# The order of TensorE's work on a strip: products and row sums in runs of four chunks instead of a change of kind with every chunk

## The reference, cut to what matters

```
XB = h @ B.T
x1 = x + tanh([h, t] @ W1 + b1) @ W2 + b2 + adj @ XB - rowsum(adj) * XB
```

## Time and profile before

| what | value |
|---|---|
| median of 3 runs | 904.75 us (904.72 to 905.37) |
| the profiled execution | 904.73 us |
| its span, first to last instruction | 903.5 us |
| TensorE matmuls busy | 776.9 us, 86% |
| VectorE busy | 729.3 us, 81% |
| DMA | 281.58 MB, mean 312 GB/s over the span |
| mean granted TensorE clock | 0.941 of full speed |

### The profile page before, as it was taken

One profiled execution on the slowest core, in us unless ns is written; L12 is line 12 of the kernel. 1 busy time (PEld: TensorE's weight loads), 2 busy tenths in 40 slices (PEclk: granted clock), 3 DMA queues, 4 the chain that ended last, 5 costly groups with the idle time before them and its releaser, 6 DMA issues.

```text
span 903.5 us, 13331 instructions
## 1 busy us (share of the span) xinstructions
PE 776.9 (86%) x5222; PEld 266.7 (30%) x5222; DVE 729.3 (81%) x958; ACT 128.5 (14%) x212; POOL 173.4 (19%) x160
## 2 busy tenths in 40 slices
PE   3898999999999999999999999999999999940000
PEld 1333232333333333333332323233333333320000
DVE  5889968989898989898989898998989897952111
ACT  2424011111111111111010201111111111110000
POOL 1000302020110202020202020202011020217774
PEclk9999999999999999999999999999999999985555
DMA  9797879697979797979798897979797979502221
GB/s 375 280 428 288 321 291 422 271 424 288 425 288 426 284 429 280 429 291 418 319 390 364 345 410 300 420 290 422 289 421 287 425 283 429 214 11 40 60 49 41
DMA packets 37267, 281.58 MB, mean 312 GB/s; under 512 B 14336, under 2 KB 18560, under 8 KB 20736
## 3 DMA queue, kind: packets, MB, share of 16 engines
q1 hardware_dynamic: 33152, 277.12, 74.9%
q0 software_dynamic: 4096, 4.20, 2.0%
HBM read 277.10 MB, written 4.19 MB: 311 GB/s over the span
## 4 chain that ended last, share of the span: by engine, by line
PE 74%; POOL 7%; DVE 5%; issue 4%; DMA 4%; SPq 4%; ACT 0%; POOLq 0%; DVEq 0%
PE acc L726 44%; PE row_sums L734 22%; POOL gathered L367 7%; DMA ring<-in_adj_t 4%; SPq L255 4%; DVE max_hi L514 2%; PE ps_hid L754 2%; PE ps_feat L796 1%; PE ps_xb L775 1%; PE ps_acc L768 1%; PE ps_turn L782 1%; PE ps_acc L771 1%; PE ps_acc L773 1%; PE ps_turn L789 1%; DVE max_lo L513 0%
## 5 line engine op out<-in xcount | busy, mean ns | idle before, releaser
L726 PE MATMUL acc<-ring,x_pb 128*64 128x512 f32 x2048 | 462.8, 601 | 18.4 <-DMA ring<-in_adj_t 18.4
L513 DVE TENSOR_TENSOR max_lo<-max_lo,ring 128x2048 f32<-128x2048 f32 x96 | 220.6, 2298 | 44.7 <-DMA ring<-in_adj_t 44.2
L734 PE MATMUL row_sums<-ring,ones_cols 128*32 128x512 f32 x2048 | 240.0, 597 | 0.0
L726 PEld LDWEIGHTS acc<-ring,x_pb 128*64 128x64 f32 x2048 | 141.0, 138 | 326.1 <-issue 326.1
L514 DVE TENSOR_TENSOR max_hi<-max_hi,ring 128x2048 f32<-128x2048 f32 x96 | 219.7, 2289 | 0.0
L358 POOL DMA_INDIRECT cand<-in_adj,cls_row x64 | 78.0, 1218 | 663.5 <-DVE cls_row L543 648.9
L734 PEld LDWEIGHTS row_sums<-ring,ones_cols 128*32 128x32 f32 x2048 | 56.5, 109 | 151.6 <-issue 149.8
L367 POOL DMA_INDIRECT gathered<-feats_dram,best x64 | 62.8, 981 | 19.5 <-issue 19.5
L651 DVE TENSOR_TENSOR gathered<-gathered,bias_row 128x512 f32<-128x512 f32 x8 | 5.6, 703 | 67.5 <-DMA gathered<-feats_dram,best 67.5
L508 DVE TENSOR_TENSOR max_lo<-ring 128x2048 f32<-128x2048 f32 x16 | 36.7, 2292 | 4.4 <-DMA ring<-in_adj_t 2.5
L510 DVE TENSOR_TENSOR max_hi<-ring 128x2048 f32<-128x2048 f32 x16 | 36.6, 2288 | 4.2 <-DMA ring<-in_adj_t 3.9
(11 more groups left out here) (95 smaller groups left out, 423.3 us busy)
## 6 DMA issues: line engine op xcount, KB each, us to landing
ring<-in_adj_t SPq DMA_DIRECT2D x128, 2048.0 KB, 11.3
x_tq<-in_x SPq DMA_DIRECT2D x1, 2048.0 KB, 30.8
feats_dram<-feats SPq DMA_DIRECT2D x16, 128.0 KB, 2.3
out<-gathered SPq DMA_DIRECT2D x8, 256.0 KB
x_pb<-in_x SPq DMA_DIRECT2D x1, 1536.0 KB, 7.8
cand<-in_adj,cls_row POOLq DMA_INDIRECT x64
gathered<-feats_dram,best POOLq DMA_INDIRECT x64
x_pb<-in_x SPq DMA_DIRECT2D x1, 512.0 KB, 4.6
```

The lines of the kernel that those rows point to most:

```text
L513: dve.tensor_tensor(max_lo[:, :], max_lo[:, :], lo, ALU.max).then_inc(lo_done, 1)
L726: last = pe.matmul(acc[parity][at:at + D, :], x_pb[:, c * CB + b, :], slot(c)[:, b * W:(b + 1) * W], start=(c == 0 and b < 2), stop=(c == ...
L734: last = pe.matmul(row_sums[at:at + QUAD, :], ones_cols[:, :], slot(c)[:, b * W:(b + 1) * W], start=(c == 0 and b < 4), stop=(c == NC - 1 ...
```

## The change

Only the program of TensorE changes. In strips 1 to 15 it takes the kinds in runs: products of chunks 0 and 1; `turn_maxima` and `turn_sums`; sums of 0 to 3; products of 2 to 5; `turn_h1`; sums of 4 to 7; `features` and `mlp_hidden`; products of 6 and 7, next to which stand those of the next strip's 0 and 1. The wait for a chunk's arrival becomes a function of its own. A chunk is released to SP (`pe_chunk`) when its second use is issued and done, still in the order of the chunks. Strip 0 keeps its order. The loads, SP's queue, VectorE, ScalarE and GpSimd are as they were.

```diff
+            def arrived(s, c):
                 pe.wait_ge(chunk_in[c % RING], s * (16 * NC // RING) + 16 * (c // RING + 1))
+            def products(c, parity):
...
             def strip(s, parity):
-                for c in range(NC):
-                    if c == 1:
-                        turn_maxima(s - 1)
-                        turn_sums(s - 1)
-                    chunk(s, c, parity)
-                    if c == 4:
-                        turn_h1(s - 1, ps_turn)
-                    if c == 5:
-                        features(s - 1)
-                        mlp_hidden(s)
+                for c in (0, 1):
+                    arrived(s, c)
+                    products(c, parity)
+                turn_maxima(s - 1)
+                turn_sums(s - 1)
+                pe.wait_ge(rows_copied, s)
+                for c in (0, 1):
+                    sums(c).then_inc(pe_chunk, 1)
+                for c in (2, 3):
+                    arrived(s, c)
+                    sums(c)
+                for c in (2, 3):
+                    products(c, parity).then_inc(pe_chunk, 1)
+                for c in (4, 5):
+                    arrived(s, c)
+                    products(c, parity)
+                turn_h1(s - 1, ps_turn)
+                for c in (4, 5):
+                    sums(c).then_inc(pe_chunk, 1)
+                for c in (6, 7):
+                    arrived(s, c)
+                    sums(c)
+                features(s - 1)
+                mlp_hidden(s)
+                for c in (6, 7):
+                    products(c, parity).then_inc(pe_chunk, 1)
```

More of the change, by code:

```diff
@@ L718, in turn_first @@
                 last.then_inc(pro_turned, 1)
-            def products(s, c, parity):
+            def arrived(s, c):
                 pe.wait_ge(chunk_in[c % RING], s * (16 * NC // RING) + 16 * (c // RING + 1))
+            def products(c, parity):
                 for b in range(CB):
@@ L736, in sums @@
                 return last
[L738 to L749, removed]
             def mlp_hidden(s):
@@ L800, in strip @@
             def strip(s, parity):
-                for c in range(NC):
-                    if c == 1:
-                        turn_maxima(s - 1)
-                        turn_sums(s - 1)
-                    chunk(s, c, parity)
-                    if c == 4:
-                        turn_h1(s - 1, ps_turn)
-                    if c == 5:
-                        features(s - 1)
-                        mlp_hidden(s)
+                for c in (0, 1):
[24 more added lines that the diff above has]
+                    products(c, parity).then_inc(pe_chunk, 1)
             for c in range(NC):
+                arrived(0, c)
+                if c % 2:
+                    sums(c)
                 pe.wait_ge(pro_norm, c + 1)
-                chunk(0, c, 0, first=True)
+                last = products(c, 0)
+                if c % 2 == 0:
+                    last = sums(c)
+                last.then_inc(pe_chunk, 1)
                 if c == 0:
```

## The result

| | before | after |
|---|---|---|
| median | 904.74 us (4 runs) | 945.74 us (945.45 to 946.49, 4 runs) |
| ratio | | 1.0455, 95% interval 1.0436 to 1.0473 |
| profiled execution, span | 904.73, 903.5 us | 945.45, 944.2 us |
| mean granted clock | 0.941 | 0.928 |

The prediction was 942.5 us with a range of 925 to 960.

The account below looks back on a forecast made before the run. TensorE's own work was taken to bound the kernel before the change. 904.7 us plus 34.9 over 13 strip periods and 2.8 in strip 1 gave 942.4, stated as 942.5 us, range 925 to 960.

Parts of the forecast that it names:

- What bounds the kernel: Steady strips before the change: TensorE's own work sets the 47.52 us period; chunk 0 lands 1.5 us before use.
- What the change removes: TensorE's groups per strip: 11 runs become 4, 0.95 us less work a strip, 13 us over 14 strips.
- The sign I had named: Profile after the change: 13 us less TensorE work on matmuls in all.
- the walk: One steady strip timed step by step from the issue of its chunk 0 load: period 50.27 us, +2.75 a strip.
- What the change moves: Later features delay the next strip's loads: TensorE waits 2.1 us for chunk 0 and 1.3 for chunk 1.
- The sign of some 28 waits: TensorE's products wait for the ring's DMA some 28 times, 40 to 50 us more in total.
- The sum: Whole kernel: 904.7 us plus 34.9 over 13 periods and 2.8 in strip 1, giving 942.4 us.
- The clock: TensorE's granted clock in the strips: no fall, despite new idle times of 2.1 and 1.3 us.
- the two ends I had worked out: A clock fall in each strip: +0.4 us a strip (948 us) on chunk 0's products, +1.67 (966 us) if later.
- the sign of a granted clock of 1.00 in the strips: Profile after the change: TensorE's granted clock stays at full speed, 1.00, in the strips.
- The rival named for it: TensorE's matmul bursts after DMA waits start on the throttled clock: 948 to 966 us, chance 15%.
- VectorE: Rival that VectorE sets the period: 35.6 us of work, exactly in step; a loss adds tenths per strip; no chance given.

Follow-up runs that it names:

- late_store: Changed kernel with SP's store of a strip's features moved behind the load of chunk 3 of the strip after the next: 886.73 us, ratio 0.9822.
- before_late_features: Kernel before, old order kept, with features and mlp_hidden behind chunk 6 in place of chunk 5: 990.03 us, ratio 1.0944.
- filler: Changed kernel with two extra unread matmuls per strip behind the products of chunk 7, in the wait for chunk 0: 943.83 us, ratio 1.0427.
- small_between: Changed kernel with turn_maxima and turn_sums put between the products of chunk 0 and those of chunk 1: 944.7 us, ratio 1.0464.

## Why the prediction was right

**What bounds the kernel.** The loop named there, `features`, copy, store, load, chunk 0, is what sets the period after the change. It is shown by two edits that have nothing in common but this loop: SP's queue without the store ahead of the loads (-59 us) and `features` earlier (-50 us). That grouping by itself does no harm is shown by `late_store`, and that the old order becomes slow by the same cause is shown by `before_late_features`.

**What the change removes.** 13 us forecast, 13.4 measured between two kernels side by side. The sign I had named, 13 us less in all matmuls, was not seen: they take 3.9 us more (780.8 for 776.9). Of this, 12.7 us are the falls of the clock, by the products of `filler`. Without them it is 8.8 us less, and the sign itself was named too high: the walk charges two starts of a run behind the two waits, 0.28 us a strip, so its own terms give 14 x (0.95 - 0.28) = 9.4. The Trainium skill, page "TensorEngine Tiling (Array Packing)", says in "Key Properties" that a change of mode drains the engine; these times agree with a fixed cost at each change of some 0.13 to 0.14 us, and don't show what it consists of.

**What the change moves.** The walk's terms beside the rows: sums of four 7.01, measured 7.00; products of four 13.90, measured 13.88; from `features` to the load 3.15, measured 3.11; wait for chunk 0 2.1, measured 2.0 to 2.4 in strips 3 to 14; wait for chunk 1 1.3, measured 1.24. The wait for chunk 1 costs what it was said to: 1.35 us a strip between `filler` and `small_between_filler`. The sign of some 28 waits came as 19 more: nine waits for chunk 1 are gone into the falls. One term has a slip without effect: a load of chunk 4 at I + 20.7 lands by the walk's own 7.57 us at I + 28.3, not 28.6, and it is needed at I + 32.9.

**The sum.** The first loads of strips 2 and 15 are at 121.39 and 778.70: 657.3 us for 13 periods, 50.56 each, where the walk had 50.27. This is +3.8 us; the part ahead of it came out 0.4 shorter (121.39 for 121.8) and the part behind 0.4 shorter (944.2 - 778.70 = 165.5 for 165.9). 942.4 + 3.8 - 0.8 = 945.4, which is the profiled execution's time. Of the 3.8 us some 2.0 are the falls of the clock in eight of these 13 strips, at a quarter of a microsecond each, the distance between strips with and without one (the ninth fall, in strip 15, lies behind them). The rest is that strips without a fall have 50.4 us and not 50.27: chunk 1 comes 12.4 to 12.7 us behind the issue where the walk had 12.47.

**The clock.** Here the value taken was wrong: I took no fall, and there were nine. Of the two ends I had worked out, the mild one holds in the changed kernel (+0.4 forecast for a strip where P0 takes it, 0.25 measured, the wait for chunk 1 covering the rest). So the sign of a granted clock of 1.00 in the strips failed (0.98), and the number hardly felt it; that the falls stood where a wait hid them is what kept it near 942, since `small_between` pays 1.6 us for each. What failed is the reason, that 2.1 us of idle time is a little nearer to 1.34 than to 2.97. Two strips waited 2.01 us, and the clock fell in one of them; strip 2 waited 2.68 us and had no fall. Nothing that I looked at in a strip's own rows tells which, and it stays open. The rival named for it, bursts that begin cold after a wait for a transfer (the Trainium skill, "TensorE: Matmul & The Clock Gate", section "HAM oscillation — how this bites in real kernels"), was true in nine of 14 strips here, in ten of `small_between`, and in all of `before_late_features`; in the last two it cost some 17 and 13 us. Of the two falls that I had said agree with it, only the first stood behind a transfer; the second stood behind a copy of ScalarE.

**VectorE** did not become the bound. It was forecast exactly in step, and has some slack: 0.57 us of idle time before chunk 0 in the strip at 432, as this row of its timeline shows.

```profile
432.04 2.29 DVE L508 TENSOR_TENSOR max_lo<-ring 128x2048 f32<-128x2048 f32 x1 [0.57 <-DMA ring<-in_adj_t]
```

**The best kernel** of the study is `late_store`, 1.8% faster than the kernel before: the change together with the cure for what it collides with.

## What to carry to other kernels

When work is moved on an engine, look at what the moved group releases, and follow it through every queue to the next transfer: here 3.4 us of row sums ahead of one small group delayed a store, and behind it in SP's queue the loads. A slack read from the trace (1.5 us between a landing and its use) is the first number to compare with such a shift. And put a wait that can be late behind all loads that cannot wait.

## What the runs showed of the hardware that was not expected

- Idle times of 2.0 to 3.3 us on TensorE brought the granted clock to half in nine of 14 strips of the changed kernel, and 2.2 to 3.5 us in ten of `small_between`; idle times of 2.01 to 2.68 us in the other strips did not. 3.6 us and more did so in every strip of `before_late_features`. With 0.2 to 0.8 us before chunk 0 and 1.2 before chunk 1 (`filler`) there was no fall in the strips.
- A fall costs 1.5 to 1.7 us on 16 product instructions (5.18 to 5.35 us for 3.65), and 3.0 where the clock stayed down longer (6.62), unless a wait follows. With the wait for chunk 1 behind it only about 0.25 us were left of it, with that for h1 some 0.5.
- Matmuls that nobody reads can so make a kernel faster: 944.7 to 927.9 us with 30 of them.
